# Two convolution taps per product from a delayed copy of u, with dummy products between the spreads

## What is computed

```python
zxbcdt = u @ in_proj_w.T
xBC = zxbcdt[..., 2 * d_mlp + d_ssm:2 * d_mlp + d_ssm + conv_dim]
dt = jax.nn.softplus(dt + dt_bias)
xpad = jnp.pad(xBC, ((0, 0), (D_CONV - 1, 0), (0, 0)))
xconv = conv_b
for k in range(D_CONV):
    xconv = xconv + xpad[:, k:k + L, :] * conv_w[:, k]
xconv = silu(xconv)
xs = xconv[..., :d_ssm]
Bm = xconv[..., d_ssm:d_ssm + D_STATE]
Cm = xconv[..., d_ssm + D_STATE:]
```

## Time and profile before

| | us |
|---|---|
| median of 3 runs | 68.89 |
| lowest and highest | 68.42, 71.41 |
| the profiled execution | 68.96 |
| its span, first to last instruction | 67.2 |
| mean granted TensorE clock in it | 0.941 |

### The profile page before, as it was taken

How to read it: one execution, slowest core, us unless ns; L and a number is a source line. 1 busy time by engine, 2 the same in 40 slices (tenths; PEclk the granted TensorE clock), 3 DMA queues, 4 the chain that set the end, 5 groups by cost and what they waited for, 6 DMA issues and landing times.

```text
span 67.2 us, 2423 instructions
## 1 busy us (share of the span) xinstructions
PE 56.7 (84%) x1018; PEld 34.7 (52%) x1018; DVE 50.5 (75%) x133; ACT 36.2 (54%) x82; POOL 25.5 (38%) x61
## 2 busy tenths in 40 slices
PE   2996769999999989999999999947558999995900
PEld 0334268545848347549569946614147344494600
DVE  2054694895389998999999687399875879999740
ACT  0454199944695990358876005932995804568000
POOL 5987478780004101036999786000006032000000
PEclk9999999559999999999999999999999658999996
DMA  0899910000000000000000000000000000000045
GB/s 0 274 336 312 396 65 0 10 0 0 0 0 0 5 0 10 0 5 10 0 10 0 0 10 0 10 0 0 0 0 5 10 0 0 0 0 0 10 146 166
DMA packets 2011, 3.00 MB, mean 45 GB/s; under 512 B 208, under 2 KB 1232, under 8 KB 2000
## 3 DMA queue, kind: packets, MB, share of 16 engines
q1 hardware_dynamic: 1424, 1.83, 8.4%
q10 hardware_dynamic: 576, 1.02, 4.2%
HBM read 2.32 MB, written 0.52 MB: 42 GB/s over the span
## 4 chain that ended last, share of the span: by engine, by line
PE 64%; DVE 13%; ACT 9%; DMA 5%; issue 3%; DVEq 1%; SPq 1%; ACTq 0%
PE ps L298 9%; PE ps L338 8%; PE ps L506 5%; DMA vc<-vec_in 5%; PE ps L427 5%; PE ps L620 4%; PE ps L374 3%; PE ps L321 3%; PE ps L547 3%; PE ps L515 3%; PE ps L531 3%; PE ps L411 2%; PE ps L399 2%; ACT L710 2%; DVE ell L913 2%
## 5 line engine op out<-in xcount | busy, mean ns | idle before, releaser
L298 PE MATMUL ps<-zbf 128*128 128x512 bf16 x35 | 11.4, 486 | 1.3 <-DVE zbf L847 1.3
L913 DVE TENSOR_TENSOR_SCAN ell<-ps,delta 128x512 f32<-128x512 f32 x8 | 9.2, 1208 | 0.8 <-PE ps L399 0.7
L298 PEld LDWEIGHTS ps<-zbf 128*128 128x128 bf16 x35 | 4.0, 123 | 6.6 <-issue 3.3
L338 PE MATMUL ps<-u,wtap 64*32 64x256 f32 x128 | 5.4, 469 | 0.3 <-ACT bc L710 0.3
L620 PE MATMUL ps<-h,wk 64*64 64x256 bf16 x144 | 4.7, 275 | 0.9 <-DVE h L1115 0.8
L1214 POOL TENSOR_SCALAR sc<-sc 128x1 f32<-128x1 f32 x1 | 4.9, 4926 | 0.1
L620 PEld LDWEIGHTS ps<-h,wk 64*64 64x64 bf16 x144 | 3.8, 106 | 1.9 <-issue 1.5
L961 DVE TENSOR_TENSOR mm<-ell,gsb 128x1024 f32<-128x1024 f32 x4 | 4.6, 1208 | 0.0
L346 PE MATMUL ps<-u,wtap 64*64 64x512 f32 x32 | 4.5, 613 | 0.0
L506 PEld LDWEIGHTS ps<-mm,xdz 64*32 64x32 f32 x256 | 3.3, 106 | 1.3 <-issue 1.2
L745 ACT ACTIVATE ysq<-yg 128x512 f32<-128x512 f32 x2 | 1.3, 631 | 4.9 <-DVE yg L980 4.9
(11 more groups left out here) (252 smaller groups left out, 141.4 us busy)
## 6 DMA issues: line engine op xcount, KB each, us to landing
w1n<-c1n_in ACTq DMA_DIRECT2D x1, 288.0 KB, 3.9
w2t<-c2t_in SPq DMA_DIRECT2D x1, 288.0 KB, 6.4
w1t<-c1t_in SPq DMA_DIRECT2D x1, 288.0 KB, 6.7
x_sb<-x_in ACTq DMA_DIRECT2D x1, 256.0 KB, 3.4
x_sb<-x_in SPq DMA_DIRECT2D x1, 256.0 KB, 3.2
cw_sb<-cw_in SPq DMA_DIRECT2D x1, 256.0 KB, 5.9
out<-o_sb SPq DMA_DIRECT2D x1, 256.0 KB, 2.6
out<-o_sb SPq DMA_DIRECT2D x2, 128.0 KB, 1.9
```

The lines of the kernel that those rows point to most:

```text
L298: mul(ps[:, bank, :], zbf[:, 0:P], zbf[:, :], start=True, stop=True)
L338: last = mul(ps[q:q + 32, BC[j], bank_col:bank_col + TOK], wtap[half(h), k, at:at + 32], u[half(h), 2 * j + b, k:k + TOK], start=(k == 0), ...
L913: vec_.tensor_tensor_scan(dst, ps[:, SPREAD[g % 2], :], delta[:, :], 0.0, ALU.mult, ALU.add).then_inc(scanned, 1)
```

## The change

A second input `xt` is loaded: x with channels of one half (images 0 to 3, then 4 to 7) twice on the partitions, on 0 to 63 delayed by one token, on 64 to 127 as it is. From it `ut` is made as u is from x: the same scale and bias per channel. The scale and bias exist with other partitions, so two small products on PE with a duplicating matrix (K_DUP, in the constants) bring them to all 128 partitions, and DVE copies them out of PSUM to rw. `ut` has eight pieces of 128x256: two made by DVE, six by POOL, ahead of POOL's masks. When all are there DVE clears the first column of the delayed half, and only then (`ut_ready`) PE may begin.

A product now contracts over 128 rows: taps 2m and 2m + 1 at once, the weights wtap[128, 2, 128] with one tap on either row half. There are 8 products for x (16 before), and 16 each for B and for C (32 before).

The order is changed too. All of x's projection stands ahead of B's, and B's ahead of the statistics; the first four prefixes are together, behind the row parts; where the x taps stood between spreads 3 to 6 there are ten dummies; C is in one piece ahead of the seventh spread; the silu of C is ahead of the copy of the transposed B on ACT. There is one more warm-up dummy. On ACT's queue the constants come second, then half of xt, then w1n; on SP's queue the other half of xt comes behind cw, which is half as large.

```diff
-            keep_warm(5)
-
+            keep_warm(6)
+            pe.wait_ge(ld_cst, 16)
+            pe.wait_ge(nbias_ready, 1)
+            for h in range(2):
+                s = slice(CH * h, CH * h + CH)
+                last = mul(ps[:, RWB[h], 0:8], cs[s, K_DUP:K_DUP + P], rn[s, :, :].rearrange("p e b -> p (e b)"),
+                           start=True, stop=True, tile_position=(CH * h, 0))
+            last.then_inc(rw_wide, 1)
...
-            state_projection(A_B, 0).then_inc(b_proj, 1)
+            pe.wait_ge(tap_ready, 1)
+            pe.wait_ge(ut_ready, 1)
+            pe.wait_ge(ut_dve, 2)
+            for h, j, p in halves:
+                if 2 * h + j:
+                    pe.wait_ge(ut_pool, 4 * h + 2 * j)
+                for m in range(2):
+                    last = mul(ps[half(p), XS[j], :], wtap[:, m, A_XS:A_XS + CH], ut[:, h, 2 * j:2 * j + 2, 2 * m:2 * m + TOK],
+                               start=(m == 0), stop=(m == 1), tile_position=(0, CH * p))
+            last.then_inc(xs_proj, 1)
+            state_projection(A_B).then_inc(b_proj, 1)
...
             prefix(1, 0, 1, 2, 3).then_inc(prefix_sums, 1)
+            keep_warm(2, DTB)
             spread_rows(3)
-            x_projection(2)
+            keep_warm(3, DTB)
             spread_rows(4)
-            x_projection(3).then_inc(xs_proj, 1)
+            keep_warm(3, DTB)
             spread_rows(5)
+            keep_warm(2, DTB)
             pe.wait_ge(lxb_ready, 2)
             pe.wait_ge(b_silu, 1)
-            state_projection(A_C, TOK, range(0, 2))
+            state_projection(A_C).then_inc(c_proj, 1)
             spread_rows(6)
             x_to_tokens(0)
+            spread_rows(7)
             x_to_tokens(1)
-            spread_rows(7)
...
+            dve.wait_ge(rw_wide, 1)
+            vec_.tensor_copy(rw[:, :, :, :].rearrange("p h e b -> p h (e b)"), ps[:, RWB[0]:RWB[1] + 1, 0:8]).then_inc(rw_ready, 1)
+            dve.wait_ge(rw_ready, 1)
+            dve.wait_ge(ld_xt0, 16)
+            dve.wait_ge(zero_u, 1)
+            for b in range(2):
+                ts(ut[:, 0, b, 2:TP], xt_sb[:, 0, b, :], rw[:, 0, 0, b:b + 1], rw[:, 0, 1, b:b + 1], ALU.mult, ALU.add).then_inc(ut_dve, 1)
...
+            dve.wait_ge(ut_dve, 2)
+            dve.wait_ge(ut_pool, 6)
+            vec_.memset(ut[0:CH, :, :, 2:3], 0.0).then_inc(ut_ready, 1)
             dve.wait_ge(ld_w1n, 16)
...
+            pool.wait_ge(rw_ready, 1)
+            pool.wait_ge(zero_u, 1)
+            pool.wait_ge(ld_xt0, 16)
+            pool.wait_ge(ld_xt1, 16)
+            for h, b in ((0, 2), (0, 3), (1, 0), (1, 1), (1, 2), (1, 3)):
+                gp.tensor_scalar(ut[:, h, b, 2:TP], xt_sb[:, h, b, :], rw[:, h, 0, b:b + 1], rw[:, h, 1, b:b + 1],
+                                 ALU.mult, ALU.add).then_inc(ut_pool, 1)
+            pool.wait_ge(ut_pool, 6)
```

More of the change, by code:

```diff
@@ L80, with build @@
 UP = TAPS - 1 + TOK
-def build(nc, x, wa, cw, wb, vec, cst, c1n, c1t, c2t, out):
+TP = TAPS - 2 + TOK
+def build(nc, x, xt, wa, cw, wb, vec, cst, c1n, c1t, c2t, out):
     with ExitStack() as ctx:
@@ L103, in build @@
         one_row = cs[0:1, K_HALF:K_HALF + CH]
-        cw_sb = sb("cw_sb", [P, TAPS * A_TAP])
-        wtap = sb("wtap", [P, TAPS, A_TAP])
+        cw_sb = sb("cw_sb", [P, 2 * A_TAP])
+        wtap = sb("wtap", [P, 2, A_TAP])
+        xt_sb = sb("xt_sb", [P, 2, HALF_B, TOK])
+        ut = sb("ut", [P, 2, HALF_B, TP])
+        rw = sb("rw", [P, 2, 2, HALF_B])
+        rn = sb("rn", [P, 2, HALF_B])
+        rstd, nbias = rn[:, 0, :], rn[:, 1, :]
         u = sb("u", [P, HALF_B, UP])
@@ L215, in build @@
             sem(n) for n in ("ld_x0", "ld_x1", "ld_wa", "ld_cw", "ld_vec", "ld_cst", "ld_wb"))
+        ld_xt0, ld_xt1, rw_wide, rw_ready, ut_dve, ut_pool, ut_ready = (
+            sem(n) for n in ("ld_xt0", "ld_xt1", "rw_wide", "rw_ready", "ut_dve", "ut_pool", "ut_ready"))
         ld_w1n, ld_w1t, ld_w2t = (sem(n) for n in ("ld_w1n", "ld_w1t", "ld_w2t"))
@@ L328, in half, with state_projection @@
                 return slice(CH * p, CH * p + CH)
[L330 to L334, removed]
+            def state_projection(at):
+                for m in range(2):
                     for h, j, p in halves:
@@ L337, in state_projection @@
                             q = 32 * (2 * p + b)
-                            last = mul(ps[q:q + 32, BC[j], bank_col:bank_col + TOK], wtap[half(h), k, at:at + 32],
-                                       u[half(h), 2 * j + b, k:k + TOK], start=(k == 0), stop=(k == TAPS - 1),
-                                       tile_position=(CH * h, q))
-                return last
[L343 to L348, removed]
-            state_projection(A_B, 0).then_inc(b_proj, 1)
+                            last = mul(ps[q:q + 32, BC[j], TOK * (at == A_C):TOK * (at == A_C) + TOK], wtap[:, m, at:at + 32],
+                                       ut[:, h, 2 * j + b, 2 * m:2 * m + TOK], start=(m == 0), stop=(m == 1), tile_position=(0, q))
+                return last
+            pe.wait_ge(tap_ready, 1)
[4 more added lines that the diff above has]
+                    pe.wait_ge(ut_pool, 4 * h + 2 * j)
+                for m in range(2):
+                    last = mul(ps[half(p), XS[j], :], wtap[:, m, A_XS:A_XS + CH], ut[:, h, 2 * j:2 * j + 2, 2 * m:2 * m + TOK],
+                               start=(m == 0), stop=(m == 1), tile_position=(0, CH * p))
+            last.then_inc(xs_proj, 1)
+            state_projection(A_B).then_inc(b_proj, 1)
             pe.wait_ge(var_ready, 1)
@@ L387, in _ @@
             last.then_inc(row_ready, 1)
-            prefix(0, 2, 3).then_inc(prefix_sums, 1)
+            pe.wait_ge(dt_wide, 1)
+            prefix(0, 0, 1, 2, 3).then_inc(prefix_sums, 1)
             def spread_rows(g):
@@ L637, in _ @@
             act.dma_start(x_sb[:, 2:4, :], x[:, 2:4, :]).then_inc(ld_x1, 16)
+            act.dma_start(cs[:, :], cst).then_inc(ld_cst, 16)
+            act.dma_start(xt_sb[:, 1, :, :], xt[:, 1, :, :]).then_inc(ld_xt1, 16)
             act.dma_start(w1n[:, :], c1n).then_inc(ld_w1n, 16)
[L639 removed]
             act.dma_start(wb_sb[:, :], wb).then_inc(ld_wb, 16)
@@ L1253, in constants, with tap_pairs @@
     return c
+def tap_pairs(x):
+    x = x.reshape(2, HALF_B, CH, TOK).transpose(2, 0, 1, 3)
+    o = np.zeros((2, CH, 2, HALF_B, TOK), np.float32)
+    o[0, :, :, :, 1:] = x[:, :, :, :-1]
+    o[1] = x
+    return o.reshape(P, 2, HALF_B, TOK)
 def twice(w):
```

30 lines of the change are left out of this document (12 added, 18 removed).

## The result

The changed kernel takes 78.68 us (median of 4 runs, 77.82 to 79.40) against 68.87 before: a ratio of 1.141, 95% interval 1.126 to 1.156. The forecast was 74.9 with a range of 72.3 to 79.0: the sign holds, and so does the range, by 0.3 us for the median (one run, 79.40, lies above it); the size was 6.0 us where 9 to 10 came. The profiled execution is the 77.82 us one, its span 76.1 (67.2 before).

The account below looks back on a forecast made before the run. PE was taken to bound the kernel up to the scans, DVE through them. Terms: 68.96 + 2.1 (head) + 3.0 (x's place) − 0.4 (clock) + 1.2 (between spreads) = 74.9 us; range 72.3 to 79.0.

Parts of the forecast that it names:

- PE is the chain to the scans, DVE through them, and what stands ahead is paid in full: Whole kernel: a later start of the scans reaches the end at full price; only 0.42 us of idle could swallow part.
- The loads cost nothing; xt lands by 8.7: Head: the first 2.15 MB, xt included, land by 8.7 us, before rw at 9.45; loads costed at nothing.
- rival 2: PE's x projection: products run in strict program order, 3.1 us more, 78.0 in all; chance 0.06.
- rival 3: PE's projections: the clock stays low through x and B, 77.4 in all; chance 0.10.
- POOL's piece 0.50, six in 3.4 us with DVE beside it: Head: POOL's six ut pieces take 3.0 us plus 0.4 for DVE beside them; PE starts 2.1 us later.
- Rivals 1 and 4: Head: 1, POOL's pieces cost 1.26 each, 79.5, chance 0.12; 4, cheaper head and hidden dummies and C, 71.9, chance 0.10.
- Two taps per product save PE nothing: PE's projections: cost goes by columns, x stays 4.08 us; all of it ahead of the sums adds 3.0.
- Rival 5: PE's projections: full-height products cost what half-height ones did, so projections halve; 71.1 in all, chance 0.06.
- The order of the products: PE's x projection: left and right column halves overlap despite the written order, so 8 steps of 0.51, not 14.
- The clock: PE before the scans: clock falls again, costing 0.9 us where it cost 1.3 before; −0.4 us.
- DVE's dt is hidden: Before the sums: DVE's dt arithmetic ends at 17.6, PE reaches the sums near 20.5; 3 us to spare.
- Dummies and C between the spreads, +1.2: Scans: dummies and undivided C delay the seventh scan to 8.55 us after the first, from 7.03; scans end 1.2 later.

Follow-up runs that it names:

- e8: Changed kernel with 12 dummies on PE behind the dt products and 6 more once POOL has two pieces; 1.132 against the kernel before.
- e9: Changed kernel with new load order, 12 plus 6 dummies in the wait for ut, and C in two halves; 1.110 against the kernel before, median 76.29 us.
- e1: Changed kernel without the loads of xt, ut made from x_sb (output not the reference's); 1.095 against the kernel before.
- e3: Changed kernel with xt's first half ahead of cw on SP's queue and w1n moved there behind cw; 1.116 against the kernel before, median 76.87 us.
- e4: Kernel before with all four taps of x ahead of the sums and nothing else; 1.036, 70.9 and 71.0 us.
- e5: Changed kernel without its ten dummies between the spreads; 1.130 against the kernel before.
- e6: Changed kernel with C in two halves again, dummies kept, ACT's order of two copies as before; 1.128 against the kernel before.
- e2: Changed kernel with 24 dummies on PE behind the dt products, in the wait for ut; 77.59 us from one execution.

## Why the prediction was right or wrong

*PE is the chain to the scans, DVE through them, and what stands ahead is paid in full.* Right for the change itself: the stretch behind the scans kept its length within 0.3 us. It isn't a law. In e8 and e9 an earlier first scan came to the end only in part, because of PE's pause and, in e9, of C.

*The loads cost nothing; xt lands by 8.7.* This is the step that failed. It took the bytes in the order of both queues, as if nothing behind xt were served before it, and the pace of before. xt0 landed at 12.14, when 3.17 MB had been moved and not 2.2. e1 shows that the loads cost 3.2 us at PE's start. Of the 3.4 us between 8.7 and the landing some 2.7 are bytes from behind xt, served before it was complete, and 0.7 the slower pace; a better order took 1.2 off in e3. The prediction had written the risk down ("a late xt1 would add to POOL's start one to one") but carried no bound for it into the range. That the range held is luck: its upper end was set for other rivals. The size alone would even have spoken for rival 2 (78.0) or 3 (77.4), and only the traces say that it was neither.

*POOL's piece 0.50, six in 3.4 us with DVE beside it.* Right within 0.2 in sum: 3.62 here and 3.69 in e1. The lower slope was the one to take. The first two pieces, beside DVE, took 0.78 and 0.70 us, the other four 0.55 each. That is 0.4 in all, as the prediction had it, and not the 1.1 of a full stop. In e1, where the loads were over when POOL began, they took 0.86 and 0.70 beside the same DVE work, so it isn't the DMA engines. The Trainium skill (GPSIMD Engine Reference, Specifications) says that the two engines share the SBUF interfaces and contend when DVE is in a two-port mode or reads two inputs from SBUF; the trace agrees for the second piece, beside wtap with its two inputs, and doesn't show the mode of DVE's pieces of ut, beside which the first one ran. Rivals 1 and 4 fall: a piece takes neither 1.26 nor 0.31.

*Two taps per product save PE nothing.* Right, 3.67 and 3.72 us (e4, e8). Only the size was off: the whole group takes 3.65 to the next one's start and not 4.08, since the 1.02 of one tap contained the change to other products behind it (in e8 passes start every 0.43 us inside the group, and the first product of B 0.52 behind the last). So moving x cost 2.6 and not 3.0. Rival 5 falls with this.

*The order of the products.* Rival 2 falls: in e8 sixteen passes of 512 columns took 3.65 us, 8 steps of 0.46 and not 14, and two passes start together from the first step on, so that the right half's first pass runs ahead of three older ones of the left. The rule in the Trainium skill (TensorE: Matmul & The Clock Gate, The mechanism), that products start strictly in program order, differs from this where the tiles differ; the measurement decides.

*The clock.* That it falls and costs was right, the size not: not 0.9 us of loss but 1.6 (e8), since the low stretch was 6.6 us long and reached over 3 us into x. How long PE idles doesn't settle its length: it was as long in e1, where PE idled 2.5 us before x, and 10.2 us in e5, where it idled 4.8, less than the 5.5 here. In e5 the clock cost x 2.9 us (6.5 to the next group's start against 3.65), 2.0 more than the prediction's 0.9, so an execution near rival 3 does occur; the profiled one isn't it, and B ran at 2.4 GHz in both. (Rival 3's 77.4 puts +2.1 in the place of −0.4, which is 2.5 more and not the 2.1 that its text says.) That the sum of this stretch, forecast at +2.6, came out at +2.57 is luck: x's group was 0.4 cheaper, the clock 0.7 dearer, and B and the small products behind it together 0.3 cheaper.

*DVE's dt is hidden.* Right: dtp was ready at 20.1, the sums began at 23.86.

*Dummies and C between the spreads, +1.2.* Right, +1.24, with the seventh scan 8.52 us behind the first (8.55 was forecast). e5 and e6 give its two parts, 0.65 and 0.87, which overlap. The prediction gave nothing back for the half of C that is gone from PE behind the scans, and that term was wrong: y starts 0.4 us earlier behind mm, and later again in e6 and e9, where the half is back. It is what the last row of the table has won.

*Summed:* 68.96 + 5.4 + 2.6 + 1.2 − 0.3 = 77.9, the profiled 77.82 within rounding. The forecast lacks 2.9 us: 3.3 in the head, of which e1 gives 3.2 to the loads, less the 0.3 won at the end.

## What to carry to other kernels

Merging two half-height products into one full-height product saves instructions, not PE time, when the half-height ones already lie side by side in the array; the input copy it needs has to be paid by loads and by another engine. Before a new load is costed at nothing, ask how much would have landed if every entry that shares the engines were served at once, those behind it on its own and on other queues too (here 3.17 MB in place of 2.2), and carry a bound for a late landing into the range. An idle microsecond of PE in front of a dense group can be worth filling, but only up to the moment the data is there: four dummies won 1.3% in the kernel before, ten between the spreads cost 0.7 us.

## What the runs showed that was not expected

- Four more warm-up dummies make the old kernel faster than it was (0.9875): the clock stays at 2.4 GHz over B.
- PE paused 1.3 to 1.6 us between two weight loads, with no wait in the trace, in e2, e8 and e9, each time behind the 600th, whatever stood there; in five other kernels 0.4 to 1.0 us behind the 728th. Its cause wasn't found.
- Loads of 0.97 MB more ended 4.2 us later than before (w1t at 13.98 and 9.80), although at the 330 GB/s of the first four full slices of before (274 to 396) they are 2.9 us.
